# A convolution and attention block with cosine transforms: the first step of the frequency stage written as 384 columns side by side and four mean columns behind them

## What is computed

```python
freq2 = dct2(x_attn_img)
freq_mean = freq2.mean(axis=(2, 3), keepdims=True)
gate = jax.nn.sigmoid(5.0 * (jnp.abs(freq2) - freq_mean))
x_freq = idct2(freq2 * gate)
y = batchnorm(conv2d(x + x_freq, fr_w), bn2_g, bn2_b)
return jax.nn.gelu(y, approximate=False)
```

## Time and profile before

| | |
|---|---|
| runs | 8953.78, 8947.58, 8950.28 us |
| median | 8950.28 us |
| the profiled execution | 8950.57 us |
| its span, from the first to the last instruction | 8949.0 us |
| mean granted clock of PE | 0.934 |
| instructions | 261096 |
| activations of line 608 (first step's evictions) | 512, 489 ns each |
| activations of line 613 (gates) | 512, 511 ns each |
| copy of line 869 and absolute value of line 870 | 512 of each, 158 and 544 ns |
| gated, line 876 | 512, 544 ns each |

### The profile page before, as it was taken

The page is one execution under the profiler, slowest core; times in us unless marked ns, Lnnn a source line. Parts: engine busy times, 40 slices in busy tenths (PEclk is TensorE's granted clock), DMA queues, the critical chain, the costliest instruction groups (busy, mean ns, idle before and its releaser), DMA issues.

```text
span 8949.0 us, 261096 instructions
## 1 busy us (share of the span) xinstructions
PE 8138.8 (91%) x88874; PEld 6102.6 (68%) x88874; DVE 5502.8 (61%) x20355; ACT 5135.3 (57%) x16576; POOL 2579.1 (29%) x3417
## 2 busy tenths in 40 slices
PE   9998999999999999999999999999999999999930
PEld 8996666866676667666686667666766667666720
DVE  4554777467845775377746784477637774678410
ACT  5554765466644664376546674466537653666434
POOL 1111333133322333133323332133313331334200
PEclk9998998999989998899999998999999999999865
DMA  7561000200012000200020000200020002000089
GB/s 125 97 110 35 15 21 21 82 12 21 15 32 69 21 21 15 86 15 21 22 76 18 21 15 24 77 21 21 15 86 15 21 22 84 10 21 15 23 329 410
DMA packets 386935, 487.38 MB, mean 54 GB/s; under 512 B 249617, under 2 KB 352529, under 8 KB 369297
## 3 DMA queue, kind: packets, MB, share of 16 engines
q1 hardware_dynamic: 369488, 393.67, 15.4%
q0 software_dynamic: 16192, 77.49, 2.2%
HBM read 319.45 MB, written 151.66 MB: 53 GB/s over the span
## 4 chain that ended last, share of the span: by engine, by line
PE 76%; issue 14%; DMA 4%; POOL 3%; DVE 2%; ACT 1%; POOLq 1%; SPq 0%; DVEq 0%; ACTq 0%
PE ps L946 66%; PE ps L1084 5%; POOL work L467 3%; DMA AH<-y_scratch 2%; PE ps L1129 2%; PE ps L1081 2%; DMA out<-AH 1%; PE ps L1082 1%; DVE work L801 1%; POOLq L464 0%; DVE work L765 0%; DVE work L811 0%; ACT AH L656 0%; ACT work L555 0%; POOL work L425 0%
## 5 line engine op out<-in xcount | busy, mean ns | idle before, releaser
L555 ACT ACTIVATE work<-work 128x144 f32<-128x144 f32 x5120 | 2042.8, 403 | 36.1 <-issue 35.1
L946 PE MATMUL ps<-work 128*32 128x144 f32 (+4 forms) x32902 | 1758.8, 302 | 160.0 <-issue 96.1
L765 DVE CUSTOM_DVE_ANT_0 work<-ps,negbias 128x144 f32<-128x144 f32 x5120 | 1247.1, 302 | 628.1 <-issue 435.2
L801 DVE SCALAR_TENSOR_TENSOR work<-xs,lw,work 128x570 f32<-128x570 f32 (+1 forms) x2048 | 1587.2, 812 | 0.0
L946 PEld LDWEIGHTS ps<-work 128*32 128x32 f32 (+3 forms) x32902 | 1009.9, 127 | 699.3 <-issue 563.1
L433 POOL TENSOR_TENSOR work<-work 128x80 f32<-128x80 f32 x1024 | 482.7, 471 | 3301.8 <-DVE work L772 3301.8
L946 PE MATMUL ps<-work,wqkv 128*128 128x288 f32 x4096 | 1319.4, 447 | 98.1 <-POOL work L448 78.9
L436 POOL TENSOR_TENSOR work<-work 128x640 f32<-128x640 f32 x1024 | 1309.1, 1278 | 0.0
L946 PEld LDWEIGHTS ps<-work,wqkv 128*128 128x128 f32 x4096 | 734.2, 197 | 382.9 <-POOL work L425 83.3
L555 ACT ACTIVATION_READ_ACCUMULATOR work<-work 128x1 f32 x5120 | 971.0, 190 | 0.0
L946 PE MATMUL ps<-wproj,work 128*96 128x256 f32 x3072 | 825.7, 393 | 0.0
(11 more groups left out here) (126 smaller groups left out, 11588.2 us busy)
## 6 DMA issues: line engine op xcount, KB each, us to landing
work<-in_x SPq DMA_DIRECT2D x128, 576.0 KB, 5.5
xs<-in_x SPq DMA_DIRECT2D x64, 1152.0 KB, 5.3
AH<-in_x SPq DMA_DIRECT2D x192, 384.0 KB, 3.4
y_scratch<-AH SPq DMA_DIRECT2D x192, 384.0 KB, 2.6
AH<-y_scratch SPq DMA_DIRECT2D x64, 1152.0 KB, 24.0
out<-AH POOLq DMA_DIRECT2D x64, 1152.0 KB, 17.0
xs<-in_x SPq DMA_DIRECT2D x112, 96.0 KB, 5.1
bias_scratch<-in_rpb_rev POOLq DMA_DIRECT2D x144, 4.5 KB, 2.1
```

Of the source, the lines that this page charges most:

```text
L555: o = act.activation(sp[t % 4][:, c, :], sp[t % 4][:, c, :], ACT.Exp, scale=-1.0, bias=mn[t % 4][:, c:c + 1], accum_out=den[t % 4][:, c:c ...
L765: v.tensor_tensor_reduce(out=sp[t % 4][:, c, :], in0=psS[c], in1=negbias[:, t % 2, c, :], scale=1.0, scalar=BIG, op0=ALU.add, op1=ALU.min, ...
L801: v.scalar_tensor_tensor(dst[:, ct, :, w0:w1], xs[side][:, ct, y0 + dy:y0 + dy + HS, w0 + dx - 1:w1 + dx - 1], lw[:, ct, tap:tap + 1], dst ...
L946: return nc.tensor.matmul(o, l, r, start=start, stop=stop)
```

## The change

The tile b1 becomes a flat row of 388 elements. The eviction is two activations: one moves the 4 x 96 transformed columns, closed up, to columns 0 to 383, the other moves the four mean columns to 384 to 387 and raises the semaphore. f2 reads 384 columns in one run, and four that lie side by side. Size and place of the tile stay as they were, and so do all waits.

```diff
-        b1 = [carve("f", 4, 97) for _ in range(2)]
+        b1 = [carve("f", 388) for _ in range(2)]
...
                 def b1_out(q, par):
                     act.wait_ge(S["f1"], b * NCH + q + 1)
-                    act.activation(b1[par][0:96], ps[0:96, par, 0:388].rearrange("p (c l) -> p c l", l=97),
+                    f1 = ps[0:96, par, 0:388].rearrange("p (c l) -> p c l", l=97)
+                    act.activation(b1[par][0:96, 0:384].rearrange("p (c l) -> p c l", l=96), f1[:, :, 0:96], ACT.Copy)
+                    act.activation(b1[par][0:96, 384:388], f1[:, :, 96:97].rearrange("p c l -> p (c l)"),
                                    ACT.Copy).then_inc(S["b1_ready"], 1)
...
-                    mmul(ps[0:96, 2 + q % 2, 0:384], dct[:, 0:96], b1[q % 2][0:96, :, 0:96])
-                    mmul(ps[0:96, 2 + q % 2, 384:388], meanm[:], b1[q % 2][0:96, :, 96]).then_inc(S["f2"], 1)
+                    mmul(ps[0:96, 2 + q % 2, 0:384], dct[:, 0:96], b1[q % 2][0:96, 0:384])
+                    mmul(ps[0:96, 2 + q % 2, 384:388], meanm[:], b1[q % 2][0:96, 384:388]).then_inc(S["f2"], 1)
```

## The result

The changed kernel takes 8911.73 us in the median (8893.06 to 8929.63 over six runs) against 8953.58 for the one before on the same chip.

The account below looks back on a forecast made before the run. TensorE bounds the span (91% busy); a frequency step is closed by f2, centre, gated. Reads 0, running steps covered, ramps 8 x 0.20 = 1.6 us: forecast 8952.0 us, range 8938 to 8968.

Parts of the forecast that it names:

- The reads: In f2, reading 384 columns side by side and four neighbouring mean columns: 0 each, at most 0.05 us per step gained.
- The eviction in two: On ACT, the first part stays at 0.49 us; the second takes 0.20, moving ACT on by 0.10 (0 to 0.36).
- What hides it: In a running step, the 0.10 us delay is covered: b1_ready by 1.5 us, gate by 0.39, h_out by 0.64.
- The open ramp: At each stage's start, two evictions lie on an uncovered chain: 0.20 us per stage, 1.6 us over eight stages.
- the clock ramp falls differently: Rival: later stage ramps redraw the half-clock steps; beyond 18 us, chance 0.05 faster and 0.08 slower.
- a redraw: Another number of half-clock steps in the stage ramps; the range allowed 11.8 us either way.
- the slower side: Clock rival's slower case in the stage ramps: over 18 us more, chance 0.08; all stages like the longest, 65 us more.
- the bound: All eight frequency stages as short as the shortest: 8 x 147.66 = 1181.3 us, 62 us less.
- The two mechanical rivals: Strided reads that had cost time in f2, and a gate too late for DVE; chance 0.08 together.
- slow reads: Rival in f2: mean columns 97 apart had held it up; 0.05 us per full-clock step, 24 us faster, 8928; chance 0.04.
- a late gate: Rival between gate and gated: second part exceeds ACT's 0.39 us cover by 0.10 per step, 47 us slower, 8999; chance 0.04.

Follow-up runs that it names:

- the first experiments: Four runs against the kernel before: both evictions in old places, 0.9957; read alone, 0.9998; two evictions in each stage's first three steps only, 0.9953; only after those, 1.0001.
- the second and the fourth experiment: Kernel before: second, only f2's read of neighbouring columns changed, 0.9998; fourth, one eviction for first three steps of each stage, two in old places after, 1.0001.
- the filled gaps: Kernel before with early table load and added products ahead of PE's last strip wait, in the ramp and around the last two i1: 8833.58 us, 0.9879.
- the run with three copies: Kernel before with three one-element ACT copies ahead of each of the first three evictions of a stage: 8928.54 us, 0.9979.

## Why the prediction was wrong

**The reads: right.** I took 0 for 384 columns side by side and for the four mean columns; the run with the read alone gives 0.9998.

**The eviction in two: right in kind, too dear.** I priced the second part at 0.20 us, of which 0.10 would hold up ACT. It takes 0.16 and holds up the gate by 0.05. One of the rows behind the price I had misread: line 514, 203 ns, is the square root of one element and not a copy.

**What hides it: right.** The run with two parts after the ramp gives 1.0001; b1_ready, the gate and h_out have the cover that I read from the earlier trace rows.

**The open ramp: right in kind.** I expected 2 x 0.10 = 0.20 us per stage and it is 0.12, some 1.0 us in all instead of 1.6.

**The step that failed is the rival "the clock ramp falls differently".** I named the mechanism and the later ramp that would set it off, and then gave it 0.05 for a large gain, by this sentence: "A redraw of eight independent stages would mostly cancel, and the three runs lie within 6.2 us although nothing ties their ramps together." Both halves were wrong. The ramps are not independent draws: of the 24 with one eviction 19 fall 7.4 to 8.1 us after the first f1, 13 of them in one narrow band behind an edge, so that a shift of 0.12 us carries most of these 13 across it the same way and they do not cancel. What keeps the ramps so alike is not shown. And three runs were too few to tell a spread: the 23 runs of the kernel before beside the first experiments reach from 8920.33 to 8978.46. From these three runs came the 11.8 us that the range gave to a redraw, where the measured shift is some 42. I also held the slower side for the likelier one (0.08), "where the longer ramp pushes a little"; the longer ramp moved the time the other way. The sizes stood in my own rows: 147.66 and 163.48 us for the same work at 0.98 and 0.87. A gain of 42 us was well inside the 62 us that I had worked out as the bound, and a range that took that bound seriously would have held it.

**The two mechanical rivals**, slow reads and a late gate, are refuted by the second and the fourth experiment (0.9998 and 1.0001).

## What to carry to other kernels

Where stages with the same busy times differ by their granted clock, look for PE's idle time shortly before the fall, and fill it or take away its cause, here a table load that one word moves. That load alone was worth 0.6% and with the filled gaps 1.2%, where the edit under study was worth 0.5. Before you credit a small edit with a small gain, move its delay to another place or change its size: a gain that shrinks and goes when the delay grows points to an edge that was crossed, and the next edit may cross it back. Compare two executions of one kernel by their time at half clock first.

## What the runs showed of the hardware

PE at half clock can stay there for 27 us although it has no idle time on record (20.48 us busy of 20.48 in the third window of the second stage), and whether it stays for 6.8 or for 27.3 us went in all 27 ramps of the two kinds with less than 20 ns of the time from the copy of the third means to the fall (up to 0.554 us, from 0.573 us on). In a ramp at full clock an idle time of PE of 1.6 us was enough for the clock to fall; with 0.60 or 0.30 us it stayed at 1.00 through the ramp. A copy of 96 x 4 elements from PSUM takes ACT 160 ns, less than the 192 ns of the copies of one element in SBUF (128 x 1, in the run with three copies), and costs the instruction behind it only 0.05 us.
